# Adding two stored copies of the expert sums: VectorE instructions against accumulating DMAs of GpSimdE

## The reference, cut to what matters

```python
x = x + _layernorm(_L0_attn_ref(_layernorm(x, axis=-1), ...), axis=-1)
x = x + _layernorm(_L0_ffn_ref(_layernorm(x, axis=-1), ...), axis=-1)

def _layernorm(x, axis=-1, eps=1e-05):
    m = jnp.mean(x, axis=axis, keepdims=True)
    v = jnp.var(x, axis=axis, keepdims=True)
    return (x - m) / jnp.sqrt(v + eps)
```

## Time and profile before

| what | value |
|---|---|
| time, median of 3 runs | 1391.33 us (1388.62 to 1393.0) |
| time of the profiled execution | 1390.42 us |
| its span, first to last instruction | 1387.4 us |
| last scatter of the experts issued | 1340.58 us |
| first DVE instruction of the closing stage | 1349.61 us |
| DVE busy from 1349.60 to 1376.96 us | 27.05 of 27.36 us |
| DMA engines busy from 1350 to 1367 us | 102.1% of 16 engines, 417 GB/s |

### The profile page before, as it was taken

How to read it: one execution, slowest core, us unless ns; L and a number is a source line. 1 busy time by engine, 2 the same in 40 slices (tenths; PEclk the granted TensorE clock), 3 DMA queues, 4 the chain that set the end, 5 groups by cost and what they waited for, 6 DMA issues and landing times.

```text
span 1387.4 us, 26788 instructions
## 1 busy us (share of the span) xinstructions
PE 1307.1 (94%) x8603; PEld 1144.5 (82%) x8603; DVE 1109.4 (80%) x3652; ACT 854.4 (62%) x2322; POOL 793.6 (57%) x1054
## 2 busy tenths in 40 slices
PE   7999999999999999999999999999999999798850
PEld 5898999999999999999999999999999988654420
DVE  7778787889788987998788978897889888654438
ACT  6677666666666666666566666666666665543324
POOL 5666565556555655556555656565556554746544
PEclk9999999999999999999999999999999999899975
DMA  9200000100010001000100001000100017999986
GB/s 294 67 1 16 1 17 9 43 16 17 2 43 24 17 1 43 24 1 17 43 24 1 16 19 32 16 17 9 36 24 17 1 35 219 270 264 289 273 256 268
DMA packets 50506, 96.48 MB, mean 70 GB/s; under 512 B 4705, under 2 KB 36930, under 8 KB 50370
## 3 DMA queue, kind: packets, MB, share of 16 engines
q1 hardware_dynamic: 44226, 85.33, 19.2%
q0 software_dynamic: 6144, 9.44, 3.3%
HBM read 68.27 MB, written 26.49 MB: 68 GB/s over the span
## 4 chain that ended last, share of the span: by engine, by line
PE 84%; DVE 5%; POOL 4%; DMA 3%; issue 3%; ACT 1%; POOLq 0%; DVEq 0%
PE bank_t L716 18%; PE bank_s L716 17%; PE bank_o L716 16%; PE bank_y L716 13%; PE bank_f L716 8%; PE bank_t L802 4%; PE bank_s L802 4%; POOL ffn_sums L2166 2%; PE bank_f L802 2%; DMA ffn_sums<-dsum,idx_s 2%; POOL xg L2153 1%; DVE fstat L1927 1%; DVE fa L1922 1%; DVE fa L1947 1%; DMA stage<-in_wq 0%
## 5 line engine op out<-in xcount | busy, mean ns | idle before, releaser
L1995 POOL TENSOR_TENSOR prob<-prob,rinv 128x512 f32<-128x512 f32 (+3 forms) x512 | 362.2, 725 | 250.6 <-DVE rinv L1534 250.2
L1130 ACT ACTIVATE prob<-prob,negmax 128x512 f32<-128x512 f32 (+3 forms) x512 | 283.2, 555 | 19.7 <-DVE negmax L1521 13.7
L1982 POOL TENSOR_TENSOR q_l<-q_sum,q_h 128x128 fp32r<-128x128 f32 x254 | 182.7, 740 | 107.7 <-ACT q_h L1110 104.9
L716 PE MATMUL bank_y<-wo_h,o_h 128*128 128x256 f32 x508 | 145.6, 287 | 0.6 <-DVE o_l L1548 0.6
L716 PE MATMUL bank_y<-wo_l,o_h 128*128 128x256 f32 x508 | 141.8, 279 | 0.0
L716 PE MATMUL bank_y<-wo_h,o_l 128*128 128x256 f32 x508 | 141.7, 279 | 0.0
L1143 ACT ACTIVATE pt_h<-bank_t 128x256 fp32r<-128x256 f32 (+3 forms) x208 | 89.7, 431 | 80.6 <-PE bank_t L802 73.1
L1143 ACT ACTIVATE pt_h<-bank_s 128x512 fp32r<-128x512 f32 (+3 forms) x203 | 88.0, 434 | 79.4 <-PE bank_s L802 74.0
L716 PE MATMUL bank_o<-pt_h,v_h 128*128 128x256 f32 x380 | 135.0, 355 | 0.7 <-DVE o_l L1548 0.7
L716 PE MATMUL bank_o<-pt_l,v_h 128*128 128x256 f32 x380 | 135.2, 356 | 0.0
L716 PE MATMUL bank_o<-pt_h,v_l 128*128 128x256 f32 x380 | 134.6, 354 | 0.0
(11 more groups left out here) (475 smaller groups left out, 4062.9 us busy)
## 6 DMA issues: line engine op xcount, KB each, us to landing
w_gu<-in_w_in SPq DMA_DIRECT2D x32, 704.0 KB
w_dn<-in_w_out SPq DMA_DIRECT2D x32, 320.0 KB
xio<-in_x SPq DMA_DIRECT2D x16, 512.0 KB, 4.6
token_table<-rows SPq DMA_DIRECT2D x8, 640.0 KB, 3.7
ffn_sums<-keys SPq DMA_DIRECT2D x4, 1024.0 KB
x_rows<-xio SPq DMA_DIRECT2D x8, 512.0 KB, 2.9
ffn_sums<-ytr SPq DMA_DIRECT2D x16, 256.0 KB, 2.5
fx<-x_rows SPq DMA_DIRECT2D x8, 512.0 KB
```

What stands on the lines that cost most here:

```text
L716: return pe.matmul(o, l, r, start=start, stop=stop, skip_group_check=True)
L1130: act.activation(p_, p_, ACT.Exp, bias=negmax[:, r, i:i + 1], scale=-1.0, accum_out=rsum[:, r, i:i + 1]).then_inc(exp_made, 1)
L1982: pool.tensor_tensor(l_[:, cols], sum_of(step)[:, cols], plain(h_)[:, cols], ALU.subtract).then_inc(pos_low, 1)
L1995: pool.tensor_tensor(p_, p_, rinv[:, r, i:i + 1].to_broadcast([P, (i + 1) * P]), ALU.mult).then_inc(prob_made, 1)
```

## The change

The tile `fb` and DVE's `add_sums` go. SP loads only copy 0, to `fa[b]`. POOL, when the load of `fa[b]` has landed (`dma_f[b]`), issues a DMA that reads copy 1 of batch b from HBM and adds it to `fa[b]` in SBUF (`accum_op`), on a semaphore of its own, `dma_add[b]`; DVE's `statistics(b)` waits for that. Four such DMAs are issued before the first inverse root, and each of the other four stands between two inverse roots. SP's loads of batches 2 to 7 still wait for `dma_s[1]`.

```diff
+        AHEAD_ADDS = 3
...
-        at[0] = weights_at
-        fb = [place(f"fb{b}", [P, TT, E], F32) for b in range(NB)]
-        assert at[0] <= weights_end
...
+        dma_add = [sem(f"dma_add{b}") for b in range(NB)]
...
-            def load_sums(b, copy):
-                sp.dma_start((fa, fb)[copy][b][:], sum_runs[copy][b]).then_inc(dma_f[b], 16)
+            def load_sums(b):
+                sp.dma_start(fa[b][:], sum_runs[0][b]).then_inc(dma_f[b], 16)
...
             AHEAD_SUMS = 2
-            for copy in range(2):
-                sp.wait_ge(dma_s[copy], 16 * (NP // 2))
-                for b in range(AHEAD_SUMS):
-                    load_sums(b, copy)
+            sp.wait_ge(dma_s[0], 16 * (NP // 2))
+            for b in range(AHEAD_SUMS):
+                load_sums(b)
+            sp.wait_ge(dma_s[1], 16 * (NP // 2))
             for b in range(AHEAD_SUMS, NB):
-                for copy in range(2):
-                    load_sums(b, copy)
+                load_sums(b)
...
-            def add_sums(b):
-                dve.wait_ge(dma_f[b], 32)
-                dve.tensor_tensor(fa[b][:], fa[b][:], fb[b][:], ALU.add).then_inc(sum_dve, 1)
-
             def statistics(b):
-                dve.wait_ge(sum_dve, b + 1)
+                dve.wait_ge(dma_add[b], 16)
...
             for b in range(NB):
-                add_sums(b)
                 statistics(b)
...
+            def add_second_copy(b):
+                pool.wait_ge(dma_f[b], 16)
+                pool.dma_start(fa[b][:], sum_runs[1][b], accum_op=ALU.add).then_inc(dma_add[b], 16)
+
+            pool.wait_ge(dma_s[1], 16 * (NP // 2))
+            for b in range(AHEAD_ADDS):
+                add_second_copy(b)
             for b in range(NB):
+                if b + AHEAD_ADDS < NB:
+                    add_second_copy(b + AHEAD_ADDS)
                 inverse_root(fmv[b % 2], fnw[b], TT)
```

More of the change, by code:

```diff
@@ L284, in build @@
             sem(f"e_{n}") for n in ("same_made", "target_made", "second_made", "same_in"))
-        sum_dve, stats_made, bias_made, final_normed, final_made = (
-            sem(n) for n in ("sum_dve", "stats_made", "bias_made", "final_normed", "final_made"))
+        stats_made, bias_made, final_normed, final_made = (
+            sem(n) for n in ("stats_made", "bias_made", "final_normed", "final_made"))
         vec_step, pool_step = sem("vec_step"), sem("pool_step")
```

## The result

The changed kernel takes 1394.16 us (median of 12 runs) where the kernel before, on the same chip, takes 1388.49 (12 runs). The ratio is 1.0039, 95% interval 1.0026 to 1.0052: 5.4 us slower. The forecast was 1395, 0.3% slower: the direction is right and the size nearly so, but the way there is only half of what I had written. In the profiled execution the span is 1394.8 us against 1387.4. I cut the closing stage at three instants, in both kernels: the issue of the last scatter, the first statistics (L1927 before, L1921 after) and the last statistics.

The account below looks back on a forecast made before the run. DVE was taken to bound the kernel, with the DMA engines 6% behind. Accumulating at 3.9 us a batch puts the last statistics at 1380.7 instead of 1376.96, 3.8 us late; on the median 1391.33 that is 1395 us, range 1387 to 1403.

Parts of the forecast that it names:

- The bound moves from DVE to the DMA engines: Closing stage: DMA engines need 3.9 us a batch against DVE's 2.91, so DVE waits about 1 us each; chance 0.50.
- The price of a row: DMA engines: an accumulated 4 KB row costs 0.33 us, two plain rows and a small surcharge, against 0.16 plain.
- with a cost by bytes: Rival, the adder is the limit: 0.42 us a row, pace 4.6 us, loss 9.7 us, 1401 us; chance 0.20.
- One row for one row: SP's and POOL's queues alternate on each engine: 8 x (0.33 + 0.16) = 3.9 us a batch.
- The rival in which POOL's queue gets more than half: Stores are put off until after the adds, so nothing changes, 1391 us; chance 0.06.
- The start: First accumulating packets 2.0 us after POOL's issue, at 1348.5; last scatter's issue to first statistics 12.9 us.
- SP's queue has work all along: Loads pass with the first five batches, stores from about 1364 on, so each accumulated row is paid with a plain one.
- DVE's step of 2.91 us: DVE's step for one batch falls from 4.03 to 2.91 us, as an add of 1.12 us goes.
- DVE stays the bound: Rival: second read overlaps the first, 0.16 to 0.22 us a row; 1385 to 1388 us, faster; chance 0.20 (or near it).
- The same 10.44 us at the end: From the last statistics to the end of the kernel the time stays 10.44 us, as before the change.
- POOL costs nothing: POOL's four late DMAs between inverse roots are covered by 5 us, and its inverse roots get rather shorter.
- The rival by which DVE's instructions hold up POOL's DMAs: Rival, POOL is the limit: descriptor waits make late adds later, time up by up to some us; chance 0.04.

Follow-up runs that it names:

- the copying kernel: Changed kernel with POOL's DMAs only copying the second copy to a tile of its own, left out of the output: 1389.16 us, 1.0010 of the kernel before.
- the held loads: Changed kernel with SP's loads of batches 2 to 7 waiting until batch 0's add has landed: 1394.88 us, 1.0056 of the kernel before.
- the divided kernels: Kernel before with DVE adding only the first two, four or five batches, POOL's DMAs the later ones: 1.0018, 0.9996, 0.9991 of the kernel before.
- four by DVE: Kernel before with batches 0 to 3 added by DVE, 4 to 7 by POOL's DMAs, bias ahead of residual: 0.9996 of the kernel before.
- those that issue them earlier: Divisions with five and four adds by DVE, each late add issued one inverse root earlier, its load moved ahead: 1.0009 and 1.0010 of the kernel before.
- five adds by DVE: Kernel before with batches 0 to 4 added by DVE, 5 to 7 by POOL's DMAs, bias ahead of residual: 0.9991 of the kernel before.

## Why the prediction was right, and what in it was wrong

**The bound moves from DVE to the DMA engines: right at the start, for the first batches and for the last.** The engines are at 0.92 to 1.05 up to the last statistics, and DVE waits for them; the copying kernel, some 4 us faster, shows that most of the loss hangs on the price of the add. In the middle the loop of 3.44 us sets the step.

**The price of a row, 0.33 us: right,** from the middle of a scatter and the plain rows. Measured 0.33 against 0.16 for the same DMA without the add, a ratio of 2.1; the rivals with a cheap second read (0.16 to 0.22) and with a cost by bytes (0.42) fall. By the Trainium skill ("Collectives: The Full Stack", the section on the bandwidth ceiling and the fold count) an add needs two source reads, with 1.93 for a reduction against a copy; the trace agrees within a tenth, on a ratio that the page has from whole collectives.

**One row for one row: right,** 179 to 179. It agrees with the Trainium skill ("DMA: Bandwidth & Descriptors", the section on queues, rings and completion order), by which an engine goes round its queues packet by packet; the page's packet can hold several descriptors, the view's are single pieces of 4 KB, and equal counts don't tell the two apart. The first batches come 3.8 us apart, forecast 3.9. The rival in which POOL's queue gets more than half falls.

**The start: wrong, the largest error.** The failed step is "from POOL's issue to the first packet I take the scatter issued at 1338.44 ... 2.0 us after the issue". That scatter found engines which were idle at its turn (slice 22 begins at 2.1, not 2.0); this DMA found SP's loads, and took 5.0. With it, `fa[0]` landed at 1348.8, 6.4 us after the scatter's issue instead of the 5.8 of the forecast, and from the first packet to the landing it took 5.2 instead of 4.9. Together 16.6 us instead of 12.9: 3.0 + 0.6 + 0.3 make the 3.7 within 0.2. That the 2.0 comes back without SP's loads is shown by the held loads.

**SP's queue has work all along: wrong.** I had the stores from 1364 on. They follow the landings, which the late start had pushed back; the first was issued at 1369.17, and its data came from 1372.7 on. So for 3.5 us the accumulated rows ran alone, at 2.6 us a batch, and the last five batches landed in 16.9 us, 3.4 each. First to last statistics 24.5 us instead of 27.2: the second error gave back 2.7 us of the first.

**DVE's step of 2.91 us: wrong, and without effect on the number.** I had subtracted 1.12 from 4.03 and not asked what ACT then does. The loop of bias, ACT and residual allows 3.44. It showed in the middle of the kernel after, and it makes the rival "DVE stays the bound" worth less than I wrote: at 0.16 us a row I had 6.6 us won, and the copying kernel, which is that case, wins nothing.

**The same 10.44 us at the end: 0.9 short.** Of the 11.32 us, 0.34 come before the last pair of DVE's sums (DVE waits 0.24 us for ACT, since the loop runs closer to ACT's end), 0.54 behind them, in the last stores. What lengthens these I have not tried.

**POOL costs nothing: right.** L1995 takes 0.23 us against the 1.11 of L2002. POOL's late DMAs made no one wait in the kernel after; in the divided kernels (up to 1.7 us of DVE with four by DVE), and most in those that issue them earlier, they do, by a load that is not there yet. The rival by which DVE's instructions hold up POOL's DMAs falls: in the kernel after, L2172 took 0.84 to 1.08 us in the four issued beside an idle DVE and 0.90 to 0.92 in the four later ones, and with five adds by DVE the DMA issued at 1357.99, in the middle of an add of DVE (1357.34 to 1358.53), had its first packet after 1.8 us, as with an idle DVE. The trace thus shows nothing of the starving of descriptors that the Trainium skill ("SBUF — State Buffer", the part on the shared port pair) warns of.

The sum of 3.8 us was thus 3.7 too little at the start, 2.7 too much in the middle and 0.9 too little at the end: 5.7, measured 5.6 by the stage. That the 1395 stands so near to 1394.16 is luck in two ways: the errors of the sum partly cancel, and the median of 3 runs that it was added to, 1391.33, lies 2.8 us above that of 12 runs, 1388.49.

## What to carry to other kernels

An add that moves from a compute engine into a DMA is paid in rows of the DMA engines, at twice a plain row, and in a transfer that must now come after the one it adds to; it can pay only where these engines have idle time at the moment of the adds, so ask for their share stage by stage before and after. Here even the divided kernels, which put the adds nearer to such a time, did not get clear of the noise. When an engine is relieved of work, follow the loop of the engines that hand each other the same tile: the removed time comes back only up to the next cycle of waits, here 0.59 of 1.12 us. A latency read from a quiet stretch of the trace can be too low by half; for a start, look for the same kind of DMA issued while another queue holds as many loads.

## What was not expected of the hardware

A DMA of GpSimdE took 1.8 to 2.1 us from issue to its first packets with the engines quiet, and 3.4 to 5.0 with four or more of SyncE's loads waiting, although the two queues then alternate packet by packet. With the engines just as full (1.02 to 1.04) but only one or two loads waiting, it took 1.8 and 2.3 us. This points to a delay before the packets are in the queue, and one that grows with the other queue's loads. Which part of it stretches (the writing of descriptors, or their reading by busy engines) no run here tells apart. SyncE's queue shows something like it: the store issued at 1369.17 into engines full of accumulating rows had its first data 3.6 us later. The instruction itself took POOL 0.92 us (median) with the add, 0.60 without.
